# Two weight-sum DMAs moved among a field's gathers, and twelve transposes and five operand sums moved in VectorE's order, in a DLRM tower kernel

## The reference

```python
e = jnp.stack([tbl_0[ids[:, 0]], ..., tbl_7[ids[:, 7]]], axis=1)      # 512 x 8 x 1024
t = jnp.tanh(jax.nn.relu(x_not @ Wn1 + bn1) @ Wn2 + bn2)              # fields not_idx
iv = field_vectors.at[:, not_idx, :].set(t)
v = jnp.concatenate([iv[:, pairs[:, 0]], iv[:, pairs[:, 1]]], axis=-1)
pair_out = jax.nn.relu(v @ W1 + b1) @ W2 + b2                         # and_pairs, or_pairs
z = (and_out.sum(1) + or_out.sum(1) + rest) / count
h = relu(concat([z, dense_ctx]) @ W_top1 + b_top1); h = relu(h @ W_top2 + b_top2); y = h @ W_top3
```

## Time and profile before

| what | value |
|---|---|
| median of 3 runs | 553.89 us (548.62 to 556.87) |
| the profiled execution | 548.29 us, of which the span is 546.3 us |
| TensorE busy | 530.2 us, 97% of the span |
| VectorE, ScalarE, GpSimd busy | 356.7, 248.6, 234.7 us |
| granted TensorE clock, mean | 0.994 |

### The profile page before, as it was taken

One profiled execution on the slowest core, in us unless ns is written; L12 is line 12 of the kernel. 1 busy time (PEld: TensorE's weight loads), 2 busy tenths in 40 slices (PEclk: granted clock), 3 DMA queues, 4 the chain that ended last, 5 costly groups with the idle time before them and its releaser, 6 DMA issues.

```text
span 546.3 us, 6174 instructions
## 1 busy us (share of the span) xinstructions
PE 530.2 (97%) x2392; PEld 440.5 (81%) x2392; DVE 356.7 (65%) x370; ACT 248.6 (45%) x301; POOL 234.7 (43%) x176
## 2 busy tenths in 40 slices
PE   5999989987999999999999999999999999999998
PEld 5988878765888888888888888888888888888885
DVE  6487997968876775888547678742332874245832
ACT  3584666515456644442537444323243432142343
POOL 5548887898117653140087017655445300000000
PEclk9999999997999999999999999999999999999999
DMA  8966956456965675366199425999999972331000
GB/s 268 324 136 146 218 150 209 136 122 146 193 124 170 144 138 167 78 108 123 39 205 319 123 93 176 276 247 247 247 247 247 246 254 79 116 92 40 0 1 0
DMA packets 38607, 87.31 MB, mean 160 GB/s; under 512 B 4305, under 2 KB 4561, under 8 KB 38578
## 3 DMA queue, kind: packets, MB, share of 16 engines
q0 software_dynamic: 18624, 49.29, 41.5%
q1 hardware_dynamic: 19522, 37.51, 21.5%
q10 hardware_dynamic: 432, 0.11, 0.1%
HBM read 86.90 MB, written 0.00 MB: 159 GB/s over the span
## 4 chain that ended last, share of the span: by engine, by line
PE 79%; POOL 13%; issue 3%; DMA 2%; ACT 2%; DVE 1%; ACTq 0%
PE PS L1070 76%; POOL XR L490 12%; POOL WR L512 1%; DMA WR<-weights 1%; DMA XR<-table,rows 1%; PE PS L1248 1%; PE PS L1099 1%; PE PS L1220 1%; ACT WO L598 1%; DMA XR<-ints 0%; PE PS L1255 0%; ACT XR L732 0%; ACT XR L657 0%; DVE WO L804 0%; POOL XR L479 0%
## 5 line engine op out<-in xcount | busy, mean ns | idle before, releaser
L1070 PE MATMUL PS<-XO,WO 128*128 128x512 f32 (+1 forms) x2256 | 508.1, 387 | 8.2 <-DVE WO L804 8.2
L1070 PEld LDWEIGHTS PS<-XO,WO 128*128 128x128 f32 x2256 | 419.7, 189 | 94.3 <-DVE WO L804 9.7
L598 ACT ACTIVATE WO<-WR 128x1024 fp32r<-128x1024 f32 x93 | 98.6, 1060 | 242.0 <-PE PS L1070 226.1
L804 DVE TENSOR_TENSOR WO<-WR,WO 128x1024 fp32r<-128x1024 f32 x93 | 113.9, 1224 | 144.7 <-ACT WO L598 144.5
L490 POOL DMA_INDIRECT XR<-table,rows x96 | 130.3, 1357 | 61.1 <-issue 28.3
L628 ACT ACTIVATE XO<-XR 128x1024 fp32r<-128x1024 f32 (+1 forms) x76 | 79.3, 1045 | 3.2 <-DVE XR L949 3.2
L512 POOL DMA_DIRECT2D WR<-weights x30 | 37.5, 1627 | 86.7 <-DVE WO L804 39.8
L880 DVE TENSOR_TENSOR XO<-XR,XO 128x1024 fp32r<-128x1024 f32 x60 | 73.1, 1220 | 1.0 <-ACT XO L628 0.9
L575 POOL DMA_INDIRECT XR<-table,rows_rest x32 | 52.4, 1638 | 40.2 <-DMA XR<-table,rows_rest 38.0
L897 DVE STREAM_TRANSPOSE XR<-XR 128x1024 f32<-128x1024 f32 x26 | 55.8, 2153 | 3.1 <-DMA XR<-table,rows 3.1
L949 DVE TENSOR_TENSOR XR<-XR 128x1024 f32<-128x1024 f32 (+1 forms) x32 | 38.5, 1216 | 0.0
(11 more groups left out here) (72 smaller groups left out, 113.4 us busy)
## 6 DMA issues: line engine op xcount, KB each, us to landing
WR<-weights SPq DMA_DIRECT2D x71, 512.0 KB, 4.8
WR<-weights POOLq DMA_DIRECT2D x30, 512.0 KB, 7.0
XR<-table,rows POOLq DMA_INDIRECT x110, 4.2
XR<-table,rows_rest POOLq DMA_INDIRECT x32, 12.7
XR<-dense_t SPq DMA_DIRECT2D x3, 32.0 KB, 2.9
XR<-w_dense SPq DMA_DIRECT2D x3, 32.0 KB, 3.1
XR<-ints SPq DMA_DIRECT2D x1, 84.0 KB, 2.1
XR<-identity ACTq DMA_DIRECT2D x1, 64.0 KB, 3.5
```

Source lines behind the costliest of these rows:

```text
L598: nc.scalar.activation(WO[:, n % 2, 0, :], WR[:, slot, :], ACT.Copy).then_inc(w_hi, 1)
L804: V_.tensor_tensor(WO[:, n % 2, 1, :], WR[:, raw_slot(n), :], WO[:, n % 2, 0, :].bitcast(FP32), ALU.subtract).then_inc(w_lo, 1)
L1070: mm = nc.tensor.matmul(PS[:, bank, cols], WO_t[:, slot, ws, i, k, :], XO[:, x0 + k, xs, cols], start=first and k == 0 and n == 0, stop=la ...
```

## The change

Three things are moved, and nothing is added or removed. The first add of stage 1's Q5 goes after the fourth gather of field 4's first half; the second stays after the eighth. The transposes of fields 2, 3 and 4 take later places. Five of stage 1's operand sums (S1.1, S3.0, S3.1, S2.1, S4.0) take later places, S1.0, S2.0 and S4.1 keep their count of t. ScalarE and VectorE read the table of buffer numbers at t = 52 instead of 50.

```diff
@@ SUMS_AT
-    (1, S1, 0): (28, 29), (1, S3, 0): (30, 31), (1, S2, 0): (32, 33), (1, S4, 0): (34, 36),
+    (1, S1, 0): (28, 30), (1, S3, 0): (32, 33), (1, S2, 0): (32, 35), (1, S4, 0): (35, 36),
@@
-SETUP_AT, REGS_AT = 44, 50
-TURNS_AT = {1: (3, 4), 2: (13, 15, 17, 19), 3: (22, 23, 25, 27), 4: (35, 37, 39, 41),
+SETUP_AT, REGS_AT = 44, 52
+TURNS_AT = {1: (3, 4), 2: (18, 18, 22, 22), 3: (25, 26, 26, 31), 4: (38, 40, 40, 48),
@@ GpSimd
-            gather_half(4, 0)
             for h in range(2):
+                gather_half(4, 0, range(4 * h, 4 * h + 4))
                 add_piece(1, Q5, h)
             gather_half(4, 1)
```

## The result

The changed kernel took 556.49 us (median of 10 runs, 554.59 to 559.51), the kernel before beside it 553.66 (10 runs, 547.96 to 562.45): ratio 1.0096, 95% interval 1.0055 to 1.0137. **Slower by 1%, within the 2% called no change**; the forecast of 544 was 12.5 us too low, and the measured time lies above the top of its range, 555. The profiled execution took 559.51 us (span 557.5).

What follows compares the result with a forecast made beforehand. TensorE was taken as the bound, with 11.97 us lost ahead of t = 44 as the ceiling. t = 44 moves from 151.35 to 145.7 (-5.6), clock +1.5: -4.1 from 548.3 gives 544.2, said 544; range 536 to 555.

Steps and rivals of the forecast that it cites:

- The waits at t = 18, 28 and 36: TensorE's three gaps of 1.62, 1.28 and 5.28 us, each ended by a VectorE weight split; all were to go.
- the stall at t = 30: A new TensorE stall of 1.1 us, because the weight split there would end at 102.4 against 101.3 wanted.
- nothing after t = 44 took the gain back: TensorE had no gap in the 132 quarters after t = 44, so the gain was to be kept.
- The table's read at t = 52: Reading the buffer table at t = 52 comes before its first use, so its effect was to be nothing.
- VectorE late for W15: At t = 30, VectorE's own queue was to start this split near 101.3 us, causing a 1.1 us stall.
- a closed row of SBUF subtractions keeps it out: A gather gets in only where VectorE idles, transposes or reads PSUM, never between back-to-back SBUF subtractions.
- the late eight gathers: Field 4's second-half gathers, let in only at VectorE's openings, were to end at 133.0 to 134.6 us against 131.96.
- Q6's add becomes the next bound: Ahead of t = 44, this add was to land at 142.6 to 144.2 us and stop TensorE 4.4 to 4.9 us.
- 1.5 of clock: Loss of 1.5 us allowed in the sum for a possible clock fall after the TensorE gap at t = 44.
- rival A: Everything won: gathers meet VectorE's openings better, Q6's add out by 129.4; 548.3 - 10.9 = 537.4 us; chance 0.22.
- rival C: Slower: one more gather heads a closed row, Q6's add at 141, clock falls again (+3.1); 552.4 us; chance 0.13.
- the allowance for slower runs: Profiled execution lay 5.6 us under its runs' median, so the new median might lie up to 5.6 higher.

Runs made afterwards that it cites:

- first kind: Groups of runs (1, 2, 6) in which the kernel before takes 542 to 545 us; no followed semaphore update over 0.2 us late in their profiles.
- after_again: The changed kernel run again unaltered, beside the kernel before: 537.46 us, ratio 0.9864.
- second kind: Groups of runs (3, 4, 5, and by its times the recorded one) in which the kernel before takes 552 to 558 us; their profiles lose update records.
- group 3: Third group of follow-up runs, with the changed kernel again and two variants of it, beside the kernel before at 552.18 us.
- before_third: The kernel before, unchanged, run once more for a profile: 559.48 us, ratio 1.0122 for the same program.
- before_again: The kernel before, unchanged, run again for a second profile: 545.27 us, ratio 0.9975.
- after_fourth: The changed kernel once more, unaltered, beside the kernel before: 552.28 us, ratio 1.0007.
- start_paced: The changed kernel with one GpSimd pause ahead of the last four gathers of field 1, against the kernel before: 551.17 us, ratio 0.9870.
- before_slow: The kernel before, unchanged, run for a profile of its own: 551.18 us, ratio 1.0009; its profiled execution took 2964.58 us.

## Why the prediction was wrong

**What held.** The waits at t = 18, 28 and 36 went, the stall at t = 30 was 1.45 to 1.62 us for 1.1, and nothing after t = 44 took the gain back in the first kind. The table's read at t = 52 cost nothing. The stall's size came out near by luck: the prediction has VectorE late for W15, and the runs show ScalarE late, behind the pair T3.1 and T3.2.

**The step that failed in the first kind** is "a closed row of SBUF subtractions keeps it out". From it came the late eight gathers and "Q6's add becomes the next bound": 4.4 to 4.9 us of gap and 1.5 of clock that never came. Gathers got in at hand-overs inside the rows, the adds for Q7 and Q6 went out from 118.4 on, the granted clock was 1.0, and the time was rival A's, 537.4. A had 0.22, because the rule was made from the worst gather of one trace. The gathers that took 1.8 to 2.0 us waited for the end of one subtraction, the three of 11 to 14 us for the end of their row. No run shows the 1.5 us that the sum has for the clock. In after_again the granted clock is 1.0 in the whole span. In the kernel before it was 0.50 from 126.4 to 132 us, and the eight quarters from 126.43 took 24.92 us (to 151.35) where eight of 2.72 are 21.76: 3.2 us, near the 3.1 that rival C adds. In the recorded profile the two stretches at half clock cost 1.68 and 1.9 us.

**The step that failed for the recorded time** is the allowance for slower runs: "if the longer runs hold something that the change does not touch, the median of the new kernel lies up to 5.6 higher". By their times, and by the changed kernel's trace beside them, they held the late updates, and the change did touch what these cost. Set after_again's span (535.8) against the recorded one (557.5): the first long row starts 6.85 us later (35.37 less 28.52); TensorE stands 6.21 ahead of 103.12; the granted clock falls with it (0.82 from 98 to 100 us, 0.50 from 100 to 104), and four quarters of 10.88 take 12.56 (1.68); the gap at t = 30 is 0.17 longer; 0.90 ahead of 189.24; 3.63 ahead of 307.40, and 1.9 of clock behind it (0.64 granted from 308 to 312; 70 quarters of 2.72 are 190.4 and took 192.32). Together 21.3 of 21.7. The stretches and the waits without a releaser are those of the second kind. In the recorded profile the count reads 83.32, 87.16, 92.87, 102.88, 103.01 while TensorE runs to 96.91. That 552.3 in group 3 is near rival C's 552.4 is luck: nothing of C's chain (a gather at the head of a closed row, Q6's add at 141) is in the recorded profile, where that add went out by 133.0.

**Why nothing was won there.** The kernel before loses 7 us between the kinds (545 to 552), the changed one 15 (537.4 to 552.3). By the traces before_third is 6.5 us longer than before_again, 5.7 of it at the start. after_fourth is 12.4 longer than after_again: 6.5 at the start, 2.98 of stop ahead of t = 28, and 1.9 in the two quarters behind it, where the granted clock was 0.50 from 106 to 108 us. So the start costs both nearly alike, and the changed kernel also pays under the row of 24 gathers, which it issues from 66 to 101 us with none over 2 us. That the refusals break up this row in the kernel before, and so spare it late updates, fits with its 4.59 and 4.43 us gathers at 67 and 73 us and its on-time updates up to 100 us, but was only argued. What makes a group of the second kind (the chip, its neighbours, or the recording of records, which are lost only there) stays open; no kernel of these could set it.

## What to carry to other kernels

When a wait has no releaser in the profile, look at the producer's own timeline and at the times of its count: if it finished long before, the update was late (here by 6 to 9 us). Then look for an unbroken row of gathers beside it and try a pause in it: here one pause brought the start back. Check the times of the count against the ends of the work, though, and not against an even rhythm: in before_third the count has a hole of 7 us (81.66 to 89.01) because TensorE stood 2.75 us and its next quarter took 4.6, and no update was late. One very long instruction in one trace can be the tail of a distribution (here three of 184 gathers took 11 to 14 us), so price it by how often such an instruction is long over all its kind, and take a second profile of the same program before a rule is made of it. Compare two versions only within one group of runs.

## What the runs showed of the hardware

- **Late semaphore updates.** In groups of the second kind, under rows of 14 to 24 gathers 1.25 us apart, updates of TensorE's count were recorded 6 to 9 us late (in start_paced 87.34 at 96.13) and ScalarE stood up to 9.81 us; under rows of eight none was over 0.3 us late. With 32 of those gathers replaced by four plain DMAs of the same bytes, updates were on time there, and after a pause of 4.13 us in the first row the start was that of the first kind.
- **Gathers and VectorE.** A gather missed up to eleven hand-overs between SBUF subtractions (11.49, 14.14, 14.30 us). It happened only where VectorE had not stood just before (30 of 71 missed the first hand-over, against none of 113), and none that missed the first got in at a later one of the same row. The adds, which read no row numbers, had a median of 1.36 us (1.18 to 3.18 in the first trace).
- **One odd execution.** In the profiled run of before_slow TensorE took 1.32 us a matmul in place of 0.227 with a granted clock of 1.0 in the records, and ScalarE and VectorE kept their durations (249.6 and 358.5 us busy). One more run of the kernel before in that group took 2459.4 us. The cause is open:

```profile
107.39 2609.58 PE L1070 MATMUL PS<-XO,WO 128*128 128x256 f32 x1980
```
